# Counting edges with one-hot matrix products: 20 buckets of whole destination rows against 40 buckets of half rows

## What is computed

```python
# layer 0: attention (ReLU, 16 heads) and a graph convolution; edges (src -> row) plus self loops
deg = zeros(N).at[row].add(1.0)                 # row is the edge's src
norm = deg[row] ** -0.5 * deg[col] ** -0.5      # col is the edge's dst
out = segment_sum(norm[:, None] * h[col], row)  # h = x @ W.T + b
# layer 1: relational convolution, two relations
for r in range(2):
    w = (edge_type == r)
    sums = segment_sum(h[src] @ W_rel[r] * w, dst)
    cnt = segment_sum(w, dst)
    out += sums / max(cnt, 1)
```

## Time and profile before

| | |
|---|---|
| timed runs | 2359.74, 2359.83, 2362.16 us |
| median | 2359.83 us |
| profiled run | 2362.39 us, of it 2360.3 us span |
| TensorE busy | 2158.8 us (91%) |
| VectorE busy | 1278.2 us (54%) |
| GpSimd busy | 1142.4 us (48%) |
| ScalarE busy | 717.7 us (30%) |
| granted TensorE clock, mean of the span | 0.96 |

### The profile page before, as it was taken

How to read it: one execution, slowest core, us unless ns; L and a number is a source line. 1 busy time by engine, 2 the same in 40 slices (tenths; PEclk the granted TensorE clock), 3 DMA queues, 4 the chain that set the end, 5 groups by cost and what they waited for, 6 DMA issues and landing times.

```text
span 2360.3 us, 41495 instructions
## 1 busy us (share of the span) xinstructions
PE 2158.8 (91%) x16776; PEld 1474.1 (62%) x16776; DVE 1278.2 (54%) x2114; ACT 717.7 (30%) x1018; POOL 1142.4 (48%) x811
## 2 busy tenths in 40 slices
PE   6899999999989799897999979979999998985997
PEld 5455564565477566674445557756778778874675
DVE  5654535525878598985654541344554444275332
ACT  4254445535632222231022231321122122051332
POOL 6577688688756511103541585023442343622564
PEclk8999999999999899998999999989999999986999
DMA  3211232233443200004000011211010000366886
GB/s 131 90 24 40 76 100 71 73 84 90 135 117 97 95 19 19 19 22 179 19 18 27 22 42 50 78 38 54 28 46 35 27 18 28 112 224 236 155 149 111
DMA packets 91851, 176.88 MB, mean 75 GB/s; under 512 B 20921, under 2 KB 60992, under 8 KB 85286
## 3 DMA queue, kind: packets, MB, share of 16 engines
q1 hardware_dynamic: 74838, 145.63, 18.6%
q0 software_dynamic: 16848, 28.91, 7.3%
HBM read 120.83 MB, written 53.50 MB: 74 GB/s over the span
## 4 chain that ended last, share of the span: by engine, by line
PE 74%; DVE 10%; POOL 6%; issue 4%; DMA 2%; ACT 2%; DVEq 0%; SPq 0%; POOLq 0%; ACTq 0%
PE ps L478 16%; PE ps L480 16%; PE ps L481 16%; PE pt L686 4%; PE ps L670 3%; PE ps L863 3%; PE pt L863 2%; DVE RB L767 2%; DVE SR L1721 2%; DVE SR L1833 1%; POOL WR L1390 1%; PE pt L1089 1%; PE pt L670 1%; PE ps L1108 1%; PE ps L1110 1%
## 5 line engine op out<-in xcount | busy, mean ns | idle before, releaser
L478 PE MATMUL ps<-WR,RB 128*128 128x256 f16 (+2 forms) x2120 | 600.7, 283 | 30.7 <-DVE SR L1721 23.8
L480 PE MATMUL ps<-WR,RB 128*128 128x256 f16 (+2 forms) x2120 | 599.8, 283 | 0.0
L481 PE MATMUL ps<-WR,RB 128*128 128x256 f16 (+2 forms) x2120 | 599.4, 283 | 0.0
L1383 POOL TENSOR_TENSOR WR<-WR,units 128x2048 f32<-128x2048 f32 (+2 forms) x25 | 107.7, 4310 | 472.1 <-PE ps L478 453.0
L478 PE MATMUL ps<-RB,WR 128*128 128x512 f16 (+1 forms) x720 | 246.1, 342 | 16.1 <-DVE RB L430 7.4
L478 PEld LDWEIGHTS ps<-WR,RB 128*128 128x128 f16 x2120 | 209.4, 99 | 76.8 <-issue 15.8
L480 PE MATMUL ps<-RB,WR 128*128 128x512 f16 (+1 forms) x720 | 245.8, 341 | 0.0
L481 PE MATMUL ps<-RB,WR 128*128 128x512 f16 (+1 forms) x720 | 245.7, 341 | 0.0
L481 PEld LDWEIGHTS ps<-WR,RB 128*128 128x128 f16 x2120 | 209.3, 99 | 43.0 <-issue 0.8
L480 PEld LDWEIGHTS ps<-WR,RB 128*128 128x128 f16 x2120 | 209.7, 99 | 41.1 <-issue 0.8
L1450 POOL DMA_INDIRECT edges_sorted<-SR x160 | 189.3, 1183 | 55.8 <-issue 55.8
(11 more groups left out here) (341 smaller groups left out, 4263.1 us busy)
## 6 DMA issues: line engine op xcount, KB each, us to landing
WR<-in_w_moe SPq DMA_DIRECT2D x64, 256.0 KB, 3.4
moe_split<-WR SPq DMA_DIRECT2D x128, 128.0 KB, 1.8
RB<-moe_split SPq DMA_DIRECT2D x8, 2048.0 KB, 13.3
WR<-in_w_mix SPq DMA_DIRECT2D x12, 1024.0 KB
WR<-in_w_mix SPq DMA_DIRECT2D x8, 1536.0 KB
RB<-in_x SPq DMA_DIRECT2D x18, 512.0 KB, 6.3
WR<-in_w_out SPq DMA_DIRECT2D x8, 1024.0 KB
counts<-RB SPq DMA_DIRECT2D x1, 6400.0 KB, 16.5
```

The costliest lines, as they stand in the source:

```text
L478: m = nc.tensor.matmul(o, ah, bh, start=(k == 0), stop=False)
L480: nc.tensor.matmul(o, ah, bl, start=False, stop=False)
L481: m = nc.tensor.matmul(o, al, bh, start=False, stop=(k == n - 1))
L1383: ch.link(g.tensor_tensor(w, w, units[:, 2:3].to_broadcast([128, width]), ALU.mult))
```

## The change

In the diff stand, in this order: the constants, the sorting's tiles, TensorE's loop, ScalarE's loop, SyncE's new DMAs (the first two of them ahead of its first load of expert weights), and VectorE's sorting, one-hots, adds, loop and degrees. Each bucket is now a source block, a relation and one half of the destinations (below 625, or from 625 on): NBK = 40 buckets. The one-hots of the destination have 625 columns, one more of ones gives the degree. Supertiles shrink to 256 edges, and there are 118. `Bc` keeps its size and is seen as 40 rows of 640. Two supertiles (a pair of four groups) share one `hot`. The rings grow: three of one-hots (was two), three of PSUM (was two), four of `rw` (was two). The last 15 columns of each half hold no counts, so the copy to HBM takes 625 of each 640, and the last 30 columns there are zeroed early by two small DMAs. The sorting code is cut into pieces that stand between TensorE's tiles: `mark` and `count` (masks and running sums for 10 buckets at a time) and `spots`, beside the evacuations of the second pair of heads.

```diff
-ST = 512
+ST = 256
-NST = 60
-BW = NODES + 2
-OUTS_AT = [4 * (u // 3) + u % 3 for u in range(4 * NT)]
+HN, HP = NODES // 2, NP // 2
+NBK = 2 * NB
+NST = 118
+BW = HN + 1
+GK = 10
+OUTS_AT = [5 * u // 2 + 1 for u in range(4 * NT)]
...
-        mask = R1(0, F32, NB, ET, parts=EP)
-        cum = R1(25600, F32, NB * ET, parts=EP)
+        mask = R1(0, F16, NBK, ET, parts=EP)
+        cum = R1(12800, F16, NBK, ET, parts=EP)
...
             for st in range(NST):
-                s = st % 2
-                if st >= 2:
-                    pe.wait_ge(rows_out, st - 1)
-                for q in range(4):
-                    pe.wait_ge(oh_ready, st * 4 + q + 1)
-                    for off, w in ((0, 512), (512, 512), (1024, BW - 1024)):
+                s, b = st // 2 % 3, st % 3
+                if st >= 3:
+                    pe.wait_ge(rows_out, st - 2)
+                for q in range(2):
+                    pe.wait_ge(oh_ready, st * 2 + q + 1)
+                    at = st % 2 * 2 + q
+                    for off, w in ((0, 512), (512, BW - 512)):
...
             for st in range(NST):
-                act.wait_ge(oh_used, st * 4 + 4)
-                if st >= 2:
-                    act.wait_ge(b_free, st - 1)
+                act.wait_ge(oh_used, st * 2 + 2)
+                if st >= 4:
+                    act.wait_ge(b_free, st - 3)
...
+            for r in range(NREL):
+                sp.dma_start(bc_d[:, NT * r:NT * r + NT, NODES:NP], zeros).then_inc(bc_saved, 16)
...
+            sp.wait_ge(st_made, 1)
+            sp.dma_start(st_offi[0:1, :], st_col[0:NST]).then_inc(st_moved, 16)
...
+            def mark(c):
+                v.tensor_tensor(mask[:, c * GK:(c + 1) * GK], keyf.unsqueeze(1).to_broadcast([EP, GK, ET]),
+                                key_ids[:, c * GK:(c + 1) * GK].unsqueeze(2).to_broadcast([EP, GK, ET]), ALU.is_equal
+                                ).then_inc(e_mask, 1)
+            def count(c):
+                dve.wait_ge(e_mask, c + 1)
+                group = mask[:, c * GK:(c + 1) * GK].rearrange("p b t -> p (b t)")
+                ch.link(v.tensor_tensor_scan(cum[:, c * GK:(c + 1) * GK].rearrange("p b t -> p (b t)"),
+                                             group, group, 0.0, ALU.add, ALU.max))
+            def spots(c):
+                for b in range(c * GK, (c + 1) * GK):
+                    m = stt(spot[min(c, 1)][:, b - c * GK], cum[:, b], small[:, 8, b:b + 1], mask[:, b], ALU.add, ALU.mult)
+                ch.link(m)
+                if c > 0:
+                    ch.link(v.tensor_tensor(spot[0], spot[0], spot[1], ALU.add))
...
+            def place_edges(t):
+                if 1 <= t <= 4:
+                    spots(t - 1)
+                if t == 5:
+                    ch.link(v.tensor_reduce(posf, spot[0].rearrange("p b t -> p t b"), AX.X, ALU.add))
+                    v.tensor_copy(pos, posf).then_inc(e_pos, 1)
+                    supertiles()
...
-            def hot(st):
-                s = st % 2
-                if st >= 2:
-                    dve.wait_ge(oh_used, st * 4 - 4)
+            def hot(j):
+                s = j % 3
+                if j >= 3:
+                    dve.wait_ge(oh_used, 4 * j - 8)
                 v.tensor_tensor(ohs[s], iota_n[:, 0:TN].unsqueeze(1).to_broadcast([128, 4, TN]),
-                                es[:, st, :, 0].unsqueeze(2).to_broadcast([128, 4, TN]), ALU.is_equal)
+                                es[:, j, :, 0].unsqueeze(2).to_broadcast([128, 4, TN]), ALU.is_equal)
                 for q in range(4):
-                    v.tensor_scalar(ohd[s][:, q, 0:NODES], iota_n, es[:, st, q, 1:2], None,
+                    v.tensor_scalar(ohd[s][:, q, 0:HN], iota_n[:, 0:HN], es[:, j, q, 1:2], None,
                                     ALU.is_equal).then_inc(oh_ready, 1)
...
-                v.tensor_tensor(rows, rows, rw[st % 2], ALU.add).then_inc(b_free, 1)
+                v.tensor_tensor(rows, rows, rw[st % 4], ALU.add).then_inc(b_free, 1)
...
             for st in range(NST):
-                if st + 2 < NST:
-                    hot(st + 2)
+                if st % 2 == 0 and st // 2 + 2 < NST // 2:
+                    hot(st // 2 + 2)
...
-            v.memset(Bc[:, :, NODES:NODES + 2], 0.0).then_inc(deg_ready, 1)
+            ch.link(v.tensor_reduce(deg[:, 1], ends, AX.X, ALU.add))
+            v.tensor_scalar(deg[:, 0], deg[:, 1], 1.0, None, ALU.add).then_inc(deg_ready, 1)
```

More of the change, by code:

```diff
@@ L284, in build_program @@
         psh16 = ps[:, 1, :].bitcast(F16)
-        pb = [ps[:, 0:3, :].rearrange("p a b -> p (a b)"),
-              pt[:, :, :, :].rearrange("p a b c -> p (a b c)")]
+        pb = [ps[:, 0:2, :].rearrange("p a b -> p (a b)")] + [pt[:, s, :, :].rearrange("p b c -> p (b c)")
+                                                              for s in range(2)]
         edges_d = nc.dram_tensor("edges_sorted", (NST * ST, 2), F32, kind="Internal").ap()
@@ L318, in build_program @@
         e_sums = sem("e_sums")
+        e_mask, st_made, st_moved = sem("e_mask"), sem("st_made"), sem("st_moved")
         e_pos = sem("e_pos")
@@ L841, in _ @@
             pe.wait_ge(e_total, 1)
-            nc.tensor.matmul(pt[0:EP, 0, 0, 0:NB], lower[0:EP, 0:EP], small[:, 0, :], start=True, stop=True)
-            nc.tensor.matmul(pt[0:EP, 0, 1, 0:NB], ones[0:EP, 0:EP], small[:, 0, :], start=True,
+            nc.tensor.matmul(pt[0:EP, 0, 0, 0:NBK], lower[0:EP, 0:EP], small[:, 0, :], start=True, stop=True)
+            nc.tensor.matmul(pt[0:EP, 0, 1, 0:NBK], ones[0:EP, 0:EP], small[:, 0, :], start=True,
                              stop=True).then_inc(e_sums, 1)
@@ L1768, in _ @@
             ch.link(v.tensor_tensor(small[:, 4], small[:, 3], small[:, 2], ALU.subtract))
-            ch.link(stt(small[:, 5], small[:, 4], float(ST), pt[0:EP, 0, 0, 0:NB], ALU.mult, ALU.add))
+            ch.link(stt(small[:, 5], small[:, 4], float(ST), pt[0:EP, 0, 0, 0:NBK], ALU.mult, ALU.add))
             ch.link(v.tensor_tensor(small[:, 6], small[:, 5], small[:, 1], ALU.subtract))
@@ L1859, in _ @@
             dve.wait_ge(b_free, NST)
-            ends = Bc[:, :, NODES:NODES + 1].rearrange("p (i r) a -> p r (i a)", r=NREL)
-            ch.link(stt(deg[:, 0], ends[:, 0], 1.0, ends[:, 1], ALU.add, ALU.add))
-            v.memset(Bc[:, :, NODES:NODES + 2], 0.0).then_inc(deg_ready, 1)
+            ends = flat.rearrange("p (i q c) -> p i q c", q=2 * NREL, c=HP)[:, :, :, HN]
+            ch.link(v.tensor_reduce(deg[:, 1], ends, AX.X, ALU.add))
+            v.tensor_scalar(deg[:, 0], deg[:, 1], 1.0, None, ALU.add).then_inc(deg_ready, 1)
+            for s in range(2):
+                ch.link(v.memset(z[s][:, NODES:NP], 0.0))
             dve.wait_ge(dis_ready, 1)
@@ L1869, in both @@
                 dve.wait_ge(turn_done, r0 + 2 * i - 2)
-                v.tensor_tensor(z[i % 2], Bc[:, 2 * i], Bc[:, 2 * i + 1], ALU.add).then_inc(z_ready, 1)
+                real = [Bc[:, 2 * i + r].rearrange("p (h c) -> p h c", h=2)[:, :, 0:HN] for r in range(NREL)]
+                v.tensor_tensor(z[i % 2][:, 0:NODES].rearrange("p (h c) -> p h c", h=2), real[0], real[1],
+                                ALU.add).then_inc(z_ready, 1)
             def make(i):
```

111 lines of the change are left out of this document (60 added, 51 removed).

## The result

The changed kernel takes **2322.3 us** (median of 4 runs, 2320.84 to 2323.57) against 2359.78 us before; the ratio is **0.9843, 95% interval 0.9832 to 0.9855**. Forecast were 2315 us in a range of 2299 to 2345. The profiled run took 2323.56 us, of it 2321.7 us span at a mean granted clock of 0.954. What follows compares it with the profiled run before (2362.39 us). Of all executions reported in this document one, of e7, ran at a clearly lower granted clock (2347.95 us at 0.917, the others of e7 at 0.961 to 0.963), and the ratios leave it out.

A forecast was written before the change was run, and what follows sets the result against it. TensorE and VectorE, both nearly full in the counting stage, were taken as the bound. 47 us gained there, less 1 for the sorting and 1 behind the stage, made 45 us: 2315 us median, range 2299 to 2345.

The forecast's parts named there:

- The bound: Counting stage: TensorE and VectorE nearly full at once, 3.17 against 3.11 us per pair of supertiles with units.
- One-hots, 0.293 us each: Counting stage, VectorE: an `ohd` of 625 columns takes 0.293 us, against 0.455 for 1250.
- B: Counting one-hots: odd length halves the rate, `ohd` stays at 0.455 us; 2347 us, or 2326 without split losses; chance 0.08.
- C: Counting one-hots: odd length costs three quarters of the rate, `ohd` 0.78 us; slower, 2404 us; chance 0.07.
- Adds, 0.40 and 0.68: Counting stage, VectorE: an add takes 0.40 us, every second one 0.28 more for waiting on its predecessor; 1.08 a pair.
- TensorE, 1.07 and 3.17 us: Counting stage: TensorE's time per pair of supertiles, 1.07 us without units and 3.17 us with 0.8 of a unit.
- The splits: Counting stage: each GpSimd weight split costs VectorE 10.5 us; two add 9 us waiting and 2.5 us halved clock each to TensorE.
- rival E: Counting stage: deeper rings hide the splits' cost to TensorE, leaving VectorE's 170 us; 8 to 15 us better, some 2303; chance 0.1.
- Rival A: Counting stage: TensorE waits in small gaps and its clock falls to 0.85; 27 us more, 2342 us; chance 0.15.
- The sorting: Before and into the attention's first tiles: the stall moves there, between 3 us gained and 7 lost, 1 lost taken.
- rival D: Sorting: stalls the attention by its upper bound, 7 us, and another 5 for a late split; 2327 us; chance 0.1.
- Behind the stage: From the counting's end on, with degrees, `Bc` write, edge load and zeroing DMAs: 1 us lost.

The follow-up runs named there:

- e7: The changed kernel with ScalarE making scale and high part of the counting stage's weight splits, GpSimd only the low part: 2300.36 us, ratio 0.9754 to the kernel before.
- e4: The changed kernel with the first 512-column matmul of each supertile done twice: 2343.2 us, ratio 0.9922 to the kernel before.
- e2: The changed kernel with GpSimd's five pieces of the second pair of heads moved into later pairs: 2317.59 us, ratio 0.9827 to the kernel before.
- e1: The changed kernel with the two zeroing DMAs issued behind SyncE's last weight load of the stage: 2318.2 us, ratio 0.9828 to the kernel before.

## Why the prediction was right, and where its terms were off

- **The bound.** The prediction had TensorE ahead in calm stretches (3.17 us a pair against VectorE's 3.11), and held that "a split can't be caught up". The first is right, as e4 shows. The second is right for the most part: e7 shortens the holds by some 20 us (an estimate, three times the 11.75 - 4.99 us of the second split) and gains 17.4. Here the prediction was better than the theory that I formed from the profile after, that VectorE alone sets the pace.
- **One-hots, 0.293 us each.** Right to the last digit (1.17 us for four). An odd length keeps the rate, so rivals B (0.455) and C (0.78) fall. The Trainium skill (Advanced Engine Details and Errata, section VectorE Performance Modes) asks for both outermost dimensions even, or both odd and equal; 625 to 625 at 0.293 us agrees. The 75 ns fixed per instruction of the Trainium skill (Vector Engine (DVE) Microarchitecture Reference, section 5.2) do not: 0.293 less 0.163 leaves 0.13, at 625 columns as at 1250.
- **Adds, 0.40 and 0.68.** Right. VectorE's pair with units is 3.00 us, not 3.11: where a unit's evacuation stands between the two adds it fills the 0.28 us of waiting, so the pair grows by 0.05 instead of 0.33 (the evacuations at 959.73 and 966.48 in the trace are one of each kind: 3.18 us for the pair with the first, which stands ahead of both adds, 2.90 for the pair with the second).
- **TensorE, 1.07 and 3.17 us.** Right: 15.86 us for five pairs.
- **The splits.** 10.5 us each of VectorE, right (10.6). The price put on the coupling was too high: from the fourth to the fifty-second set of one-hots (839.4 to 1008.7) it takes 169.3 us where the prediction had 175. That is 152.2 of TensorE and 8.5 a split instead of 11.5. VectorE catches up behind a split at 3.00 us a pair, against TensorE's 3.17, and not at the 3.11 that the prediction had; how much of the 3 us a split this explains is not shown. The start of the stage came out 2.2 us longer than forecast and its end 1.5 shorter, so this term is the 5 us by which the stage beat its forecast of 47. It is rival E in small: E named 170 us for this stretch, which is only 5 less than 175, and yet put 8 to 15 on it.
- **Rival A (clock).** The granted clock was 0.90 and 0.91 in the windows with a split, 1.00 in the one without, and 0.91 over the whole stage (0.95 before), just above the 0.9 that was named as A's sign; A wanted 0.85 throughout. The clock did fall to half, to 0.50 in 884 to 888 us, after 4 us in which TensorE was busy for 1.7, and again in 1020 to 1025 us, where VectorE leads.
- **The sorting: the term that was off most.** "Between 3 gained and 7 lost, I take **1 lost**" measured 8.1 lost: beyond the 7, though the evacuation at 133.41 lies within the 123 to 134 us that were named as a sign. The instructions' own prices were right (e2: `spots` 12.2 us against 12, adds 5.5 against 5, reduce 2.85 against 2.9). What was off was choosing the undisturbed end of the range, and the price of the two zeroing DMAs at "at most a few us, while GpSimd would wait for `pos` anyway". They did GpSimd no harm, but they moved its pieces by 8 us (96.52 against 88.42) onto `spots`. e2 gives 7.2 us for GpSimd's pieces, e1 2.2 of these for the DMAs. The head start of 2.4 us that the prediction gave the attention isn't seen: at the evacuation that started at 140.16 before, the change is 10.0 us behind and no longer 8.1, and e2 (142.65) is 2.5 and no longer 0.9. This was rival D's mechanism, without a sign of its second part (a late split): the counting begins 9.2 us late.
- **Behind the stage.** 1 us forecast, 4.6 measured; changed kernels with a clock of 1.00 in that window have a rest that is 3 to 5 us shorter, so most or all of it goes with the dip and not with the change.

The sum: 52.4 - 9.2 - 4.6 = 38.6 against 47 - 1 - 1 = 45. Two errors of 5 and 8 us have opposite signs, and the third, 4 us, comes and goes. Without the first of them the time would lie 12 us from the forecast and not 7; that much is luck.
